# Count steps of the self pass put in pairs into TensorE's stream of f32 products, in a GraphSAGE and feed-forward kernel

## What is computed

```
def _sage_layer(h, edge_src, edge_dst, deg_inv, W_self, W_neigh, b):
    msg = h[edge_src]
    agg = jax.ops.segment_sum(msg, edge_dst, num_segments=h.shape[0])
    mean = agg * deg_inv[:, None]
    return h @ W_self + mean @ W_neigh + b
...
h = jax.nn.relu(_sage_layer(x, edge_src, edge_dst, deg_inv, W_self0, W_neigh0, b0))
out = _sage_layer(h, edge_src, edge_dst, deg_inv, W_self1, W_neigh1, b1)
...
x = x + _L0_gnn_ref(_layernorm(x, axis=-1), src, dst, ...)
x = x + _L0_ffn_ref(_layernorm(x, axis=-1)[None], L0_ffn_W_fc, L0_ffn_W_proj)[0]
```

## Time and profile before

| | |
|---|---|
| median of 3 runs | 1594.97 us (1594.46 to 1595.0) |
| the profiled execution | 1594.98 us, span 1593.2 us |
| TensorE busy | 1572.6 us, 99% of the span |
| VectorE, ScalarE, GpSimd busy | 874.8, 462.9, 140.9 us |
| TensorE's granted clock | 0.998 of full speed |
| units 1 to 9 of the self pass | 156.9 to 283.4 us of the span |

### The profile page before, as it was taken

How to read it: one execution, slowest core, us unless ns; L and a number is a source line. 1 busy time by engine, 2 the same in 40 slices (tenths; PEclk the granted TensorE clock), 3 DMA queues, 4 the chain that set the end, 5 groups by cost and what they waited for, 6 DMA issues and landing times.

```text
span 1593.2 us, 23208 instructions
## 1 busy us (share of the span) xinstructions
PE 1572.6 (99%) x7728; PEld 1331.6 (84%) x7728; DVE 874.8 (55%) x1643; ACT 462.9 (29%) x857; POOL 140.9 (9%) x279
## 2 busy tenths in 40 slices
PE   7999999999999999999999999999999999999997
PEld 5777777888888888889989899898998888888885
DVE  7777776464014224564434334343343788888878
ACT  3356665121012001122213123131231233333356
POOL 1251377000000000010000000000001000000001
PEclk9999999999999999999999999999999999999999
DMA  8323344575334545576202022031122333333313
GB/s 302 120 110 102 131 153 176 210 296 204 135 106 162 205 171 183 173 229 251 80 27 105 29 77 79 26 105 38 67 79 105 107 118 118 118 118 118 112 60 50
DMA packets 55706, 205.47 MB, mean 129 GB/s; under 512 B 5360, under 2 KB 14078, under 8 KB 50084
## 3 DMA queue, kind: packets, MB, share of 16 engines
q1 hardware_dynamic: 52772, 190.19, 33.9%
q0 software_dynamic: 2848, 14.16, 2.7%
HBM read 153.85 MB, written 52.04 MB: 129 GB/s over the span
## 4 chain that ended last, share of the span: by engine, by line
PE 97%; DVE 1%; DMA 1%; issue 0%; ACT 0%; SPq 0%; ACTq 0%; DVEq 0%
PE bank L1609 27%; PE bank L1735 27%; PE bank L1754 25%; PE bank L1684 11%; PE bank L1792 3%; PE bank L1543 2%; PE bank L1585 2%; PE bank L1811 0%; DVE w L1241 0%; DMA w_landing<-w_self 0%; DMA pr_raw<-w_proj 0%; DMA rows<-x 0%; DVE stats L1196 0%; DVE xt L1229 0%; DVE rows L1212 0%
## 5 line engine op out<-in xcount | busy, mean ns | idle before, releaser
L1609 PE MATMUL bank<-w,xt 128*128 128x512 f32 x1920 | 468.6, 397 | 2.6 <-DVE w L1241 2.6
L1735 PE MATMUL bank<-x2t,fc_w 128*128 128x384 f32 (+1 forms) x2304 | 438.4, 351 | 0.7 <-ACT relu L1003 0.7
L1735 PEld LDWEIGHTS bank<-x2t,fc_w 128*128 128x128 f32 x2304 | 411.8, 188 | 25.8 <-issue 1.0
L1609 PEld LDWEIGHTS bank<-w,xt 128*128 128x128 f32 x1920 | 353.5, 189 | 71.7 <-issue 3.0
L1754 PE MATMUL bank<-pr_w,hid 128*128 128x512 f32 (+1 forms) x1728 | 394.8, 390 | 0.0
L1754 PEld LDWEIGHTS bank<-pr_w,hid 128*128 128x128 f32 (+1 forms) x1728 | 320.7, 186 | 70.8
L1454 DVE TENSOR_TENSOR y<-y,bank 128x512 f32<-128x512 f32 (+1 forms) x144 | 98.8, 687 | 207.0 <-PE bank L1754 207.0
L998 ACT ACTIVATE pr_w<-pr_raw 128x1024 fp32r<-128x1024 f32 x64 | 67.1, 1049 | 366.2 <-PE bank L1754 362.9
L1684 PE MATMUL bank<-z,at 128*128 128x512 f32 x720 | 168.4, 392 | 0.0
L1684 PEld LDWEIGHTS bank<-z,at 128*128 128x128 f32 x720 | 133.9, 188 | 27.2
L1397 DVE TENSOR_TENSOR square<-relu 128x384 f32<-128x384 f32 (+1 forms) x96 | 56.9, 593 | 144.0 <-ACT relu L1003 144.0
(11 more groups left out here) (152 smaller groups left out, 1055.0 us busy)
## 6 DMA issues: line engine op xcount, KB each, us to landing
fc_raw<-w_fc SPq DMA_DIRECT2D x64, 512.0 KB, 4.2
pr_raw<-w_proj SPq DMA_DIRECT2D x64, 512.0 KB, 3.5
xt<-xt_dram SPq DMA_DIRECT2D x24, 1024.0 KB, 5.0
xt_dram<-xt SPq DMA_DIRECT2D x18, 1024.0 KB, 4.3
at<-at_dram SPq DMA_DIRECT2D x18, 640.0 KB, 5.4
part_dram<-rows SPq DMA_DIRECT2D x20, 512.0 KB, 3.8
rows<-part_dram SPq DMA_DIRECT2D x20, 512.0 KB, 4.3
rows<-x SPq DMA_DIRECT2D x18, 512.0 KB, 5.0
```

Source lines behind the costliest of these rows:

```text
L1609: ins = nc.tensor.matmul(bank[:, 2 * (u % 2) + q, :], xt[j][:, a, k, :], w[:, k, b, q * HALF:(q + 1) * HALF], start=(k == 0 and m == 0), s ...
L1735: ins = nc.tensor.matmul(bank[:, 4 + (c if g == 0 else j % 2), 0:n], fc_w[:, j % 2, k, a, :], x2t[g][:, k, v, c0:c0 + n], start=(k == 0 an ...
```

## The change

The steps of units 1 to 9 of the self pass are put in twos: steps 0 and 1 of a unit stand at the place of step 0, steps 2 and 3 at that of step 2, and so on. In a unit of eight steps the places are 0, 12, 24, 36 with two steps each, instead of 0, 6, ... 42. In a unit of seven they are 0, 13, 27 with two and 41 with one. The last three steps of unit 0 and those of A0 keep their places. Which product, which tile and which side a step has stays as it is.

```
-    STEP_SLOTS[_unit] = [(_from + _products * m // _steps, turn) for m, turn in enumerate(TURNS[_count:_count + _steps])]
+    STEP_SLOTS[_unit] = [(_from + _products * (m // 2 * 2 if _unit > S0 else m) // _steps, turn) for m, turn in enumerate(TURNS[_count:_count + _steps])]
```

## The result

The changed kernel takes 1599.86 us (median of 8 runs, 1598.25 to 1600.31), the one before, run beside it, 1594.99 us (8 runs). The ratio is 1.0028, with a 95% interval of 1.0018 to 1.0037: slower by 4.9 us, where +4.1 was forecast. The span of the profiled execution is 1598.1 us, the granted clock 0.998 as before.

The account below looks back on a forecast made before the run. TensorE, busy with f32 products, was taken to bound the kernel, with GpSimd almost without time to spare. The terms -2.5 + 6.2 + 0.4 = +4.1 us gave 1599.1 us, range 1593.5 to 1602.5.

Parts of the forecast that it names:

- What bounds the kernel: Whole kernel: TensorE ends last for 97% of the span, so changes to its stream in the self pass arrive one for one.
- The gain: Units 1 to 9 of the self pass: 33 places fewer, each 0.075 us, -2.5 us.
- The loss by GpSimd and the queue: 21 pairs from window 34 on: late GpSimd one-hots plus TensorE's queue work behind the wait, +6.2 us, lower bound 4.2.
- Slow loads: L481 range loads on TensorE's queue, nine second windows with them on the path: +0.4 us, bounds 0 and 1.9.
- The sum: Whole kernel: -2.5 + 6.2 + 0.4 = +4.1 us.
- the main term: Pairs from window 34 on: lateness of GpSimd's one-hots and TensorE's queue work behind the wait, +6.2 us.
- Rival 1: TensorE's queue prepares the second step during the first, so only GpSimd's lateness counts: -1.4 us, 1593.6 us, chance 0.15.
- Rival 3: GpSimd's comparisons held up by VectorE in pairs, 781 ns each: +5.6 us, 1604.7 us, chance 0.05.
- Rival 2: VectorE's keys end last at unit starts in units 2 to 5: +1.6 us more, 1600.7 us, chance 0.10.

## Why the prediction was right, point by point

**What bounds the kernel**: right. The 4.97 us of the self pass are the whole difference, and nothing behind it moved.

**The gain** (-2.5): nearly right. The twelve places of units 1 to 3 gave 0.66 us in the changed kernel and 0.62 with pairs there alone. Unit 3 gave 0.07 a place. So did units 6 and 9 with both causes of the loss removed (13.35 and 13.48 us, against 13.56 and 13.75 of the kernel before without its stalls). Thirty-three places at 0.07 less the 0.2 us of the two longer rows are about 2.1 us.

**The loss by GpSimd and the queue** (+6.2): the mechanism and its links as forecast, with these sizes. In unit 7 the copy starts 0.62 us after the first product of a pair of eight products (forecast 0.63), two blocks end 3.3 us later (3.39), and the last product starts 0.97 us after them (0.97). In unit 9, without a load, it starts 0.58 to 0.72 us after them (0.58). The waits and loads of TensorE's queue answer to the earlier trace rows:

```profile
L1564 PEldq EVENT_SEMAPHORE  x43: 51/774/1097, 200.3 to 284.1; - x43
L481 PEldq TENSOR_LOAD <-window_range x21: 327/332/1565, 201.9 to 283.3; - x21
```

What was off is the form: "the loss falls on every other pair". In the trace all pairs are late. Take x, the time from the start of a pair's first product to the start of its last one, from TensorE's timeline, as the earlier trace rows has it (the chain counts products by their ends, and puts the first one 0.16 us later):

```profile
247.13 0.52 PE L1543 MATMUL bank<-key_hot,src_hot 125*128 125x160 bf16 x5
...
248.11 0.24 PE L1543 MATMUL bank<-key_hot,src_hot 125*128 125x160 bf16 x1
...
250.98 0.66 PE L1543 MATMUL bank<-key_hot,src_hot 125*128 125x160 bf16 x7
```

In unit 7 x is 1.29, 0.98, 1.06 and 1.10 us, where 0.48 (eight products) to 0.62 (ten) is unhindered. The last product of a pair starts 0.62 + 3.32 + 0.97 = 4.91 us after the first product of the pair before, and 2.87 us of that lie between the two pairs (248.11 to 250.98). So the x of two neighbours add up to 2.04 us, whatever the first one is. Measured: 2.27, with a slow load of 0.71 us on VectorE beside it, 2.04, and 2.16 behind the pair of ten products, whose copy starts 0.14 us later. The forecast's own sum is 4.99 - 2.86 = 2.13. It began with a pair on time, at 0.50, and so got 0.50 and 1.63 in turn; in the kernel the lateness is spread. The mean is the same, and so is the loss: the four pairs of unit 7 take 2.34 us more than unhindered ones (forecast 2.3), those of unit 9 1.37 (1.5).

**Slow loads** (+0.4): the term that was mis-sized. Units 4, 6 and 8 lost 0.3 to 0.6 us more than forecast. The two visible holes are 0.60 us each, in unit 4 and in unit 8:

```profile
202.18 0.50 PE bank L1543 x7
202.69 0.60 issue
```
```profile
263.07 0.36 PE bank L1543 x5
263.43 0.60 issue
```

With the features' transfer cut down these three units are 1.6 us shorter. The bound of 1.9 held it; the value taken did not. The forecast had looked only at how often a load is slow, not at where: they stand at the starts of units, where SyncE issues its large transfers, so they are not spread over the windows by chance.

**A term left out.** The kernel before had stalls of its own, 0.8 us by the run with its queue's work ahead. The forecast read one of them, at 232, but took none off. In the changed kernel they stand inside the pairs' loss and are not paid twice.

**The sum.** Counted pair by pair in the chain against unhindered pairs (0.57, 0.71 or 0.85 us for eight, ten or twelve products), the changed kernel loses 8.0 us, of which 1.6 are the slow loads by the run above and so 6.4 GpSimd and the queue. With the gain of 2.1 and the 0.8 of the kernel before: 6.4 + 1.6 - 2.1 - 0.8 = 5.1 us, against 4.98 measured. The forecast's 4.1 is 0.9 below because the slow loads were 1.2 too low, the gain 0.4 too large and the main term 0.2 too low, while the stalls left out were worth 0.8 the other way. That this omission made up for most of the slow loads is luck; that the main term is within 0.2 us is not.

**Rival 1**, the queue's work is hidden: refuted. The last product follows GpSimd's end by 0.58 us or more in every pair of units 7 and 9, and the rival needs under 0.3. With the load, the loop and the branch gone units 1 to 9 are 4.0 us shorter; slow loads account for some 1.6 of that. **Rival 3**, GpSimd held up by VectorE: refuted, its comparisons are as the earlier trace rows (busy and mean; then ns min/median/max):

```profile
L769 POOL TENSOR_SCALAR src_hot<-iota,current 125x128 bf16<-125x128 f16 x84 | 53.6, 647 | 8.5 <-POOL current L764 8.5
L769 POOL TENSOR_SCALAR src_hot<-iota,current x84: 597/651/747, 199.3 to 284.1; 125x128 bf16<-125x128 f16 x84
```

By the rule of the Trainium skill ("SBUF — State Buffer", section "SBUF: two separate sides"), an exclusive lock with the loser waiting for the whole instruction, a comparison that lost to VectorE would wait out one of its instructions. The slowest of 84 is 0.10 us over the middle one, so this trace shows no such wait. The rule holds for VectorE only in a two-port mode or with two inputs in SBUF, and the trace doesn't show the mode, so it neither bears the rule out nor speaks against it. **Rival 2**, VectorE's keys: not as the main cause, but present in unit 5. With GpSimd and TensorE's queue both relieved, two pairs of twelve products there take 1.00 and 0.95 us against 0.85 for the others, about 0.25 us together; and where VectorE has a slow load of its own and TensorE has none it decides a pair in units 7 and 8 (the run with the turns fixed).

## What to carry to other kernels

Before two steps are put together, write down what each engine that feeds them does between the release of a buffer and the next use: with two buffers, a pair turns an engine that has just enough time (1.67 of 1.72 us) into one that is late at each pair, since its lead was the distance between the steps. Count everything that the consumer's queue does behind the wait (here 0.6 or 0.97 us of register loads, loop entry and a second wait) as part of the producer's time. And put what does not depend on the wait ahead of it: in the kernel before that edit alone took 0.8 us out of the pass (in both traces taken with it, units 6 to 9 have the same lengths). Then look at which instructions are slow now and then, and where they stand: a slow load of the range moved from queue to queue and from unit to unit with the edits here, and kept several of them from the time that was expected.

## What was not expected

A load of four numbers from SBUF into registers takes 0.33 us on TensorE's queue, but 0.92 to 1.57 us at four of 21 places of the changed kernel, always within some 4 us of a unit's start; with the 1 MB transfer of features cut to 128 KB two of these places came back to 0.33 and one fell to 0.70, while a fifth rose to 0.92. It hits VectorE's and GpSimd's queues too (1.25 us on GpSimd at 231.6). And the cost of a visit by bf16 products to the f32 stream is paid nearly once a row, however long the row: over 0.2267 us a product, rows of six take 0.05 to 0.08 us more, rows of twelve 0.07 to 0.09 (but for the two longer ones), rows of fourteen 0.08 to 0.09.
